# An oscillating memory stage with tokens on partitions: running sums as products, halves of the tokens in turn

## The chip, the cores and the metric

The kernel is one program on one core of a Trainium2 chip. A core has five engines with a queue each: TensorE (PE, matrix products into PSUM), VectorE (DVE), ScalarE (ACT, activation functions), GpSimd (POOL), and SyncE (SP), which issues the transfers here. The engines run side by side and wait for each other through semaphores. The metric is the device time of one execution in microseconds (us); less is better.

## What is computed

The network has two layers, each with a cross attention over a context, a token mixer and a mixture of experts. The stage of this change is the token mixer of the first layer, on 8 sequences of 64 tokens with 256 features:

```python
Bm = x @ W_B + b_B
Cm = x @ W_C + b_C
dt = jax.nn.softplus((x @ W_dt1 + b_dt1) @ W_dt2 + b_dt2)
omega = omega_base * dt
phi = jnp.cumsum(omega, axis=1)
content = Bm * x[..., :STATE]
cphi, sphi = (jnp.cos(phi), jnp.sin(phi))
memory_real = jnp.cumsum(content * cphi, axis=1)
memory_imag = jnp.cumsum(content * sphi, axis=1)
retrieved = Cm * (memory_real * cphi + memory_imag * sphi)
y = retrieved @ W_out + b_out + D * x
```

Its input is the layer norm of the residual stream, its result is added to that stream, and the running sums start anew with each sequence.

## The kernel before

The program is a row of stages (`program`): `xattn0`, `memory0`, `ffn0`, `xattn1`, `attn1_ffn1`. Each stage opens a `Block` in which every engine has its own straight list of instructions; between blocks all engines meet at a barrier. The residual stream `core.x` (`resid` in the trace) and its norm stay in SBUF as [128, 4, 256], with 128 tokens on the partitions and four such tiles.

`memory0` works transposed. `Norm` makes `xn`, TensorE transposes it into `xnT`, and all products give features on partitions and the 512 tokens along the free side, two chunks `c` of 128 features. So every tile of the chain (`z`, `ez`, `poly`, `phi`, `cs`, `sn`, `ci`, `cr`, `mi`, `mr`) is 128 x 1024, and biases are one number per partition. The running sums over tokens are VectorE scans (L699, L709, L715), two each, with `carry` as the factor: 1, and 0 where a sequence begins.

The order is written out by hand. TensorE: step products to t1 (L734), to z (L747), B and C (L741), then, once the cosine's square is there, 24 filler products of the identity (`core.warm`, L100), which compute nothing that is used, and the output product (L757). VectorE: bias onto z, content, then the softplus. That is max(z, 0) + log1p(exp(-|z|)), and the logarithm is a polynomial of e = exp(-|z|) in factors (e + s)^2 + o, five of them (`log1p_factors`). ScalarE makes Abs, Exp and the five squares with a ring of three buffers; VectorE multiplies them up (L688 to L694). Then come omega, the scan to phi, the reduction of phi to (-pi, pi) in six operations (L701 to L705), the products and scans of both parts, and the retrieved value `mr`, which the output product reads as its stationary operand. GpSimd makes `base`, that is D times the norm, plus the output bias, plus the residual. SyncE issues twelve transfers. A product of f32 operands shows in the trace as two records, a transpose as one.

## Time and profile before

| What | us |
|---|---|
| Median of 3 runs | 1106.91 (1106.3 to 1108.91) |
| The profiled execution | 1106.76 |
| Its span, first to last instruction | 1105.1 |
| TensorE busy, whole span | 1005.0 |
| VectorE busy, whole span | 571.0 |
| ScalarE busy, whole span | 498.9 |
| Touched stage, first DMA issue to the end of the last addition | 202.25 to 259.54 |

The span is what the instructions take; the rest of an execution's time lies around it. Busy time says how much an engine did, not whether anybody waited for it. TensorE's busy share is high over the whole span, but not in this stage, so it is the stage's own timeline that has to be read. TensorE's clock has two levels, 1.2 and 2.4 GHz; the views give it as a share of the higher one, 0.50 or 1.00, or between where a stretch holds both.

### The profile page before, as it was taken

How to read it: one execution, taken by the hardware profiler on the slowest of the kernel's cores; microseconds unless marked ns; L12 is line 12 of the kernel's file. 1: busy time of each engine (PE TensorE's matmuls, PEld its weight loads, DVE VectorE, ACT ScalarE, POOL GpSimd, SP SyncE). 2: the span in 40 equal slices, each digit the busy share in tenths (PEclk: the TensorE clock that was granted, in tenths of full speed). 3: DMA queues.
4: the chain of work that ended last, by engine and by line, in shares of the span. 5: the costliest groups of instructions: out<-in, count | busy, mean ns of one | idle time of the engine just before them, and what ended most of it. 6: DMA issues, size and time to landing. Idle time of an engine off the chain costs nothing. (4 is left out here: it accounts for less than half of the span.)

```text
span 1105.1 us, 21134 instructions
## 1 busy us (share of the span) xinstructions
PE 1005.0 (91%) x8866; PEld 858.5 (78%) x8866; DVE 571.0 (52%) x811; ACT 498.9 (45%) x744; POOL 179.2 (16%) x164
## 2 busy tenths in 40 slices
PE   8899999727789999899999999999999998959998
PEld 6788888425469985588989898989898865559997
DVE  4577776495734345665545555454646412572211
ACT  5677776322346645535444444444544313213322
POOL 2000000203414423103030312111111004110000
PEclk9999999868779999999999999999999999879999
DMA  5111200102013204111111102020300005903610
GB/s 168 32 62 46 63 24 3 44 0 62 1 55 90 94 28 153 39 39 39 39 41 36 60 16 76 0 76 2 126 24 1 1 1 162 377 11 115 230 39 20
DMA packets 49396, 68.82 MB, mean 62 GB/s; under 512 B 5792, under 2 KB 40816, under 8 KB 49328
## 3 DMA queue, kind: packets, MB, share of 16 engines
q1 hardware_dynamic: 49328, 67.83, 18.7%
q8 instruction: 53, 0.87, 0.3%
q14 instruction: 15, 0.12, 0.0%
HBM read 67.29 MB, written 0.52 MB: 61 GB/s over the span
## 5 line engine op out<-in xcount | busy, mean ns | idle before, releaser
L1380 ACT ACTIVATE e_pr<-ps,e_negmax 128x1024 f32<-128x1024 f32 x64 | 71.4, 1115 | 171.0 <-DVE e_negmax L1385 164.8
L181 PE MATMUL ps<-f_pT_hi,f_cN_hi 128*128 128x256 f32 x512 | 146.1, 285 | 2.4 <-DVE f_pT_lo L1626 2.4
L181 PE MATMUL ps<-f_pT_hi,f_cN_lo 128*128 128x256 f32 x512 | 145.5, 284 | 0.0
L181 PE MATMUL ps<-f_pT_lo,f_cN_hi 128*128 128x256 f32 x512 | 145.4, 284 | 0.0
L1626 DVE TENSOR_TENSOR f_pT_lo<-ps,f_pT_hi 128x1024 fp32r<-128x1024 f32 x64 | 78.2, 1222 | 78.0 <-ACT f_pT_hi L1581 78.0
L181 PE MATMUL ps<-e_cT_hi,e_qb_hi 128*128 128x512 f32 x256 | 105.5, 412 | 0.0
L404 DVE SCALAR_TENSOR_TENSOR a_u<-ps,a_floor,a_cap 128x1024 f32<-128x1024 f32 x64 | 79.2, 1279 | 45.9 <-PE ps L485 45.9
L181 PEld LDWEIGHTS ps<-f_pT_hi,f_cN_hi 128*128 128x128 f32 x512 | 98.5, 192 | 4.6 <-DVE f_pT_lo L1626 2.6
L181 PE MATMUL ps<-e_cT_hi,e_qb_lo 128*128 128x512 f32 x256 | 100.6, 393 | 0.0
L181 PE MATMUL ps<-e_cT_lo,e_qb_hi 128*128 128x512 f32 x256 | 99.9, 390 | 0.0
L181 PEld LDWEIGHTS ps<-f_pT_lo,f_cN_hi 128*128 128x128 f32 x512 | 98.6, 193 | 1.5
L181 PEld LDWEIGHTS ps<-f_pT_hi,f_cN_lo 128*128 128x128 f32 x512 | 98.6, 193 | 0.0
L1385 DVE TENSOR_REDUCE e_negmax<-ps 128x1 f32<-128x1024 f32 x64 | 78.1, 1220 | 30.9 <-PE ps L181 30.2
L336 ACT ACTIVATE a_pr<-a_u,a_nb 128x1024 f32<-128x1024 f32 x64 | 73.8, 1154 | 44.4 <-DVE a_u L404 43.3
L1581 ACT CAST f_pT_hi<-ps 128x1024 fp32r<-128x1024 f32 x64 | 64.8, 1013 | 53.5 <-PE ps L1654 53.5
L1654 PE MATMUL ps<-ident,e_pr 128*128 128x128 f32 x512 | 66.5, 273 | 13.5 <-DVE f_pT_lo L1626 12.3
L100 PE MATMUL ps<-ident 128*128 128x128 f32 x240 | 40.9, 349 | 35.7 <-ACT b_cs L667 19.7
L1375 POOL TENSOR_TENSOR e_cT_lo<-e_rawT,e_cT_hi 128x512 fp32r<-128x512 f32 x32 | 40.4, 1295 | 193.6 <-ACT e_cT_hi L1563 193.6
L1654 PEld LDWEIGHTS ps<-ident,e_pr 128*128 128x128 f32 x512 | 57.0, 140 | 18.5 <-issue 18.3
L100 PEld LDWEIGHTS ps<-ident 128*128 128x128 f32 x240 | 39.4, 261 | 38.7 <-ACT b_cs L667 20.6
L1549 POOL TENSOR_TENSOR f_cN_lo<-e_raw,f_cN_hi 128x512 fp32r<-128x512 f32 x32 | 43.7, 1398 | 138.5 <-ACT f_cN_hi L1570 138.5
L181 PEld LDWEIGHTS ps<-e_cT_hi,e_qb_lo 128*128 128x128 f32 x256 | 48.0, 188 | 11.1
(360 smaller groups left out, 2137.1 us busy)
## 6 DMA issues: line engine op xcount, KB each, us to landing
k_w<-in_L_ffn_W SPq DMA_DIRECT2D x22, 1024.0 KB, 10.1
a_ctxT<-in_ctxT SPq DMA_DIRECT2D x16, 512.0 KB, 3.7
d_w<-in_L_ffn_w SPq DMA_DIRECT2D x32, 256.0 KB, 2.7
e_rawT<-in_ctxT SPq DMA_DIRECT2D x8, 1024.0 KB, 5.0
e_raw<-in_ctx SPq DMA_DIRECT2D x8, 1024.0 KB, 5.6
e_wq<-in_L_xattn_w_q SPq DMA_DIRECT2D x1, 1024.0 KB, 6.2
e_wk<-in_L_xattn_w_k SPq DMA_DIRECT2D x1, 1024.0 KB, 8.7
g_wv<-in_L_xattn_w_v SPq DMA_DIRECT2D x1, 1024.0 KB, 7.8
```

Source lines behind the costliest of these rows:

```text
L100: self.nc.tensor.matmul(self.bank(bank)[:, 0:P], self.ident[:], self.ident[:], start=True, stop=True)
L181: last = nc.tensor.matmul(out, a[i], b[j], start=start and n == 0, stop=stop and n == 2, skip_group_check=skip)
L336: A.activation(pr[:, n % NP, :], u[:, n % NU, :], ACT.Square, bias=nb[:], scale=HD ** -0.5).then_inc(p_ready, 1)
L404: V.scalar_tensor_tensor(u[:, n % NU, :].rearrange("p (r w) -> p r w", r=RT), core.psum[:, 0:2048].rearrange("p (r w) -> p r w", r=RT)[:, ...
L1375: nc.gpsimd.tensor_tensor(cT[1][:, c, cols], rawT[:, c, cols], cT[0][:, c, cols].bitcast(F32), ALU.subtract).then_inc(t_lo, 1)
L1380: nc.scalar.activation(pr[:, p % NPR, :], core.ps[p % 2][:], ACT.Exp, bias=negmax[:, p:p + 1], accum_out=total[:, p:p + 1]).then_inc(exp_r ...
L1385: nc.vector.tensor_reduce(negmax[:, p:p + 1], core.ps[p % 2][:], AX, ALU.max, negate=True).then_inc(max_ready, 1)
L1549: nc.gpsimd.tensor_tensor(cN[1][:, ks, :], raw[:, ks, :], cN[0][:, ks, :].bitcast(F32), ALU.subtract).then_inc(n_lo, 1)
L1581: nc.scalar.copy(pT[0][:, g, :, P * (p % 2):P * (p % 2) + P], core.ps[2][:].rearrange("p (k n) -> p k n", n=P)).then_inc(pT_hi, 1)
L1626: nc.vector.tensor_tensor(pT[1][:, g, :, cols], core.ps[2][:].rearrange("p (k n) -> p k n", n=P), pT[0][:, g, :, cols].bitcast(F32), ALU.s ...
L1654: last = nc.tensor.transpose(core.ps[2][:, k * P:(k + 1) * P], pr[:, p % NPR, k * P:(k + 1) * P], core.ident[:])
```

## The change

The stage is written with tokens on partitions. The chain's tiles are now [128, 4, 256], and each step is done for two halves `h` of two tiles, that is 512 columns.

- The product to z takes t1 as its stationary operand. The bias is a 65th row of `wdt2`, and t1 gets a 65th row of ones. The biases of B, C and the output are products of a single row of ones with a row of biases repeated for two tiles (`bias`); they open the PSUM sums into which the projections add.
- The three running sums are products with `tri`, a triangle of ones for each of the two sequences in a tile (`running`). Scans and `carry` are gone. Results stay in PSUM and VectorE reads them there.
- Softplus: the leading coefficient goes into `gain`, which ScalarE applies inside the square. VectorE's first step multiplies by e, so the separate ones for offset and lead are gone; max(z, 0) is an operation of its own (`relu`). All squares have buffers.
- Omega and D are rows broadcast over the partitions. The last step of the cosine, 1 - 2s^2, is on ScalarE. A dummy Exp of one column stands ahead of t1 on ScalarE's queue.
- `mr` has tokens on partitions and must be transposed for the output product: four transposes and a ScalarE copy per half.
- TensorE's fillers are 3 ahead of z and 30 behind the phase sums, ahead of the sums of the sine part, not 24 behind the cosine.
- GpSimd does two wide operations for `base`, not three, and makes `tri`. SyncE again issues twelve transfers: step weights, bias rows, D and omega, then wB, wC and wout, each with a semaphore of its own.

Lines with a minus are left out of the diff, since the function of before stands above.

```diff
+        tri, ones, one, dummy = sb("tri", [P, P]), sb("ones", [1, P]), sb("one", [P, 1]), sb("dummy", [P, 1])
+        t1 = sb("t1", [RANK + 1, NT])
...
+        gain = lead ** (1 / (2 * len(factors)))
...
+        wide = lambda name: sb(name, [P, TT, D])
+        relu, ez, poly = wide("relu"), wide("ez"), wide("poly")
+        square = [wide(f"square{i}") for i in range(len(factors))]
...
+        part = lambda v, h: v[:, 2 * h:2 * h + 2, :]
+        sums = lambda i, h: core.bank(i + h).rearrange("p (j d) -> p j d", d=D)
...
+            sp.dma_start(wdt2[0:RANK, :], a["L0_attn_W_dt2"]).then_inc(dt_in, 16)
+            sp.dma_start(wdt2[RANK:RANK + 1, :], a["L0_attn_b_dt2"].partition_broadcast(1)).then_inc(dt_in, 16)
             sp.dma_start(bdt1[:], a["L0_attn_b_dt1"]).then_inc(dt_in, 16)
...
+            for i, src in enumerate(("B", "C", "out")):
+                sp.dma_start(rows[:, i, :], a["L0_attn_b_" + src].partition_broadcast(1)).then_inc(rows_in, 16)
+            for dst, src in ((skip, "D"), (omega, "omega_base")):
+                sp.dma_start(dst[:], a["L0_attn_" + src].partition_broadcast(P)).then_inc(e_in, 16)
+            for w, src, done in ((wB, "B", b_in), (wC, "C", c_in), (wout, "out", o_in)):
+                sp.dma_start(w[:], a["L0_attn_W_" + src].rearrange("(c p) o -> p c o", p=P)).then_inc(done, 16)
...
+            step(g.memset(tri[:], 1.0))
+            step(g.affine_select(out=tri[:], in_=tri[:], compare_op=ALU.is_ge, fill=0.0, base=0,
+                                 pattern=[[1, P]], channel_multiplier=-1))
+            g.memset(tri[0:T, T:P], 0.0).then_inc(rows_ready, 1)
...
+            pool.wait_ge(e_in, 32)
+            step(g.tensor_tensor(base[:], xn[:], bc(skip[:], 1, TT), ALU.mult))
+            g.tensor_tensor(base[:], base[:], x[:], ALU.add).then_inc(base_ready, 1)
...
+            A.activation(dummy[:], core.ident[:, 0:1], ACT.Exp)
+            act.wait_ge(dt_in, 64)
             act.wait_ge(t1_psum, 1)
...
+            A.activation(t1[0:RANK, :], core.bank(2)[0:RANK, :], ACT.Identity, bias=bdt1[:]).then_inc(t1_ready, 1)
+            act.wait_ge(const, len(factors) + 1)
+            for h in range(HALVES):
+                act.wait_ge(z_psum, h + 1)
+                A.activation(part(ez, h), sums(0, h), ACT.Abs).then_inc(ez_abs, 1)
+            for h in range(HALVES):
+                act.wait_ge(ez_abs, h + 1)
+                A.activation(part(ez, h), part(ez, h), ACT.Exp, scale=-1.0).then_inc(ez_ready, 1)
+                act.wait_ge(ez_ready, h + 1)
+                for i in range(len(factors)):
+                    A.activation(part(square[i], h), part(ez, h), ACT.Square, bias=shift[:, i:i + 1],
+                                 scale=gain).then_inc(square_ready, 1)
+            for h in range(HALVES):
+                act.wait_ge(r_ready, h + 1)
+                A.activation(part(sn, h), part(phi, h), ACT.Sin).then_inc(sn_ready, 1)
+                A.activation(part(half, h), part(phi, h), ACT.Sin, scale=0.5).then_inc(half_ready, 1)
+                act.wait_ge(half_ready, h + 1)
+                A.activation(part(half, h), part(half, h), ACT.Square).then_inc(half_squared, 1)
+                act.wait_ge(half_squared, h + 1)
+                A.activation(part(cs, h), part(half, h), ACT.Identity, bias=one[:], scale=-2.0).then_inc(cs_ready, 1)
+            for h in range(HALVES):
+                act.wait_ge(retT_psum, h + 1)
+                A.copy(retT[:, :, 2 * P * h:2 * P * h + 2 * P],
+                       core.bank(h).rearrange("p (c n) -> p c n", c=DC)).then_inc(retT_ready, 1)
...
+            def softplus(h):
+                for i, (_, offset) in enumerate(factors):
+                    dve.wait_ge(square_ready, N * h + i + 1)
+                    step(V.scalar_tensor_tensor(part(poly, h), part(square[i], h), offset * gain * gain,
+                                                part(ez if i == 0 else poly, h), ALU.add, ALU.mult))
+                step(V.tensor_tensor(part(poly, h), part(poly, h), part(relu, h), ALU.add))
+                V.tensor_tensor(part(poly, h), part(poly, h), bc(omega[:], 1, 2), ALU.mult).then_inc(w_ready, 1)
+            def reduce(h):
+                dve.wait_ge(phi_psum, h + 1)
+                step(V.tensor_scalar(part(turns, h), sums(2, h), 1.0 / TWO_PI, MAGIC, ALU.mult, ALU.add))
+                step(V.tensor_scalar(part(turns, h), part(turns, h), MAGIC, None, ALU.subtract))
+                for i, size in enumerate((PI_A, PI_B, PI_C)):
+                    step(V.scalar_tensor_tensor(part(phi, h), part(turns, h), -size,
+                                                sums(2, h) if i == 0 else part(phi, h), ALU.mult, ALU.add))
+                V.tensor_scalar(part(phi, h), part(phi, h), 3.1415925, -3.1415925, ALU.min, ALU.max
+                                ).then_inc(r_ready, 1)
+            def imaginary(h):
+                dve.wait_ge(sn_ready, h + 1)
+                V.tensor_tensor(part(ci, h), part(content, h), part(sn, h), ALU.mult).then_inc(ci_ready, 1)
+            def real(h):
+                dve.wait_ge(cs_ready, h + 1)
+                V.tensor_tensor(part(cr, h), part(content, h), part(cs, h), ALU.mult).then_inc(cr_ready, 1)
+            def sine_part(h):
+                dve.wait_ge(mi_psum, h + 1)
+                step(V.tensor_tensor(part(mi, h), sums(4, h), part(sn, h), ALU.mult), False)
+            def retrieve(h):
+                dve.wait_ge(mr_psum, h + 1)
+                step(V.tensor_tensor(part(mr, h), sums(0, h), part(cs, h), ALU.mult))
+                step(V.tensor_tensor(part(mr, h), part(mr, h), part(mi, h), ALU.add))
+                dve.wait_ge(c_psum, h + 1)
+                V.tensor_tensor(part(mr, h), sums(6, h), part(mr, h), ALU.mult).then_inc(ret_ready, 1)
             norm.vector(dve, step)
...
+            dve.wait_ge(e_in, 32)
+            for h in range(HALVES):
+                dve.wait_ge(ez_abs, h + 1)
+                step(V.tensor_scalar(part(relu, h), sums(0, h), 0.0, None, ALU.max), False)
+            softplus(0)
+            softplus(1)
+            for h in range(HALVES):
+                dve.wait_ge(b_psum, h + 1)
+                step(V.tensor_tensor(part(content, h), sums(4, h), part(xn, h), ALU.mult), h == 1)
+            reduce(0)
+            reduce(1)
+            imaginary(0)
+            real(0)
+            imaginary(1)
+            sine_part(0)
+            real(1)
+            retrieve(0)
+            sine_part(1)
+            retrieve(1)
             dve.wait_ge(base_ready, 1)
...
+            def tile(i, j):
+                return core.bank(i + j // 2)[:, D * (j % 2):D * (j % 2) + D]
+            def bias(bank, i):
+                t.matmul(core.bank(bank), ones[:], bc(rows[:, i, :], 1, 2), start=True,
+                         stop=False, skip_group_check=True)
+            def project(first, lhsT, w, j):
+                for c in range(DC):
+                    last = t.matmul(tile(first, j), lhsT[:, c, j * P:(j + 1) * P], w[:, c, :], start=False,
+                                    stop=c == DC - 1, skip_group_check=True)
+                return last
+            def running(first, v, h):
+                for j in (2 * h, 2 * h + 1):
+                    last = t.matmul(tile(first, j), tri[:], v[:, j, :], start=True, stop=True)
+                return last
             norm.tensor(pe)
...
+            pe.wait_ge(dt_in, 64)
             for c in range(DC):
...
+                last = t.matmul(core.bank(2)[0:RANK, :], wdt1[:, c, :], xnT[:, c, :], start=c == 0, stop=c == DC - 1)
             last.then_inc(t1_psum, 1)
...
+            pe.wait_ge(rows_ready, 3)
+            core.warm(7, 3)
+            pe.wait_ge(t1_ready, 1)
+            for j in range(TT):
+                last = t.matmul(tile(0, j), t1[:, j * P:(j + 1) * P], wdt2[:], start=True, stop=True)
+                if j % 2:
+                    last.then_inc(z_psum, 1)
+            pe.wait_ge(rows_in, 48)
+            for h in range(HALVES):
+                bias(4 + h, 0)
+                bias(6 + h, 1)
+            pe.wait_ge(b_in, 16)
+            for j in range(TT):
+                last = project(4, xnT, wB, j)
+                if j % 2:
+                    last.then_inc(b_psum, 1)
+            pe.wait_ge(c_in, 16)
+            for j in range(TT):
+                last = project(6, xnT, wC, j)
+                if j % 2:
+                    last.then_inc(c_psum, 1)
+            for h in range(HALVES):
+                pe.wait_ge(w_ready, h + 1)
+                running(2, poly, h).then_inc(phi_psum, 1)
+            core.warm(0, 30)
+            for h in range(HALVES):
+                pe.wait_ge(ci_ready, h + 1)
+                running(4, ci, h).then_inc(mi_psum, 1)
+                pe.wait_ge(cr_ready, h + 1)
+                running(0, cr, h).then_inc(mr_psum, 1)
+            for h in range(HALVES):
+                bias(2 + h, 2)
+            pe.wait_ge(o_in, 16)
+            def transposes(h):
+                pe.wait_ge(ret_ready, h + 1)
                 for c in range(DC):
...
+                    for j in range(2):
+                        last = t.transpose(core.bank(h)[:, P * (2 * c + j):P * (2 * c + j) + P],
+                                           mr[:, 2 * h + j, c * P:(c + 1) * P], core.ident[:])
+                last.then_inc(retT_psum, 1)
+            def output(h):
+                pe.wait_ge(retT_ready, h + 1)
+                for j in (2 * h, 2 * h + 1):
+                    last = project(2, retT, wout, j)
+                last.then_inc(y_psum, 1)
+            for h in range(HALVES):
+                transposes(h)
+                output(h)
```

On TensorE, from the t1 product on, the order before was this (`b_wdt` is W_dt1 or W_dt2, `ident` with no second name a filler):

```order
L734 MATMUL ps<-xnT,b_wdt 64x512
L747 MATMUL ps<-b_t,b_wdt 128x512 [waits b_t1_ready]
L747 MATMUL ps<-b_t,b_wdt 128x512
L741 MATMUL ps<-xnT,b_wB 128x512 [waits b_w_in]
L741 MATMUL ps<-xnT,b_wB 128x512 x3
L741 MATMUL ps<-xnT,b_wC 128x512 x4
L100 MATMUL ps<-ident 128x128 [waits b_half_squared]
L100 MATMUL ps<-ident 128x128 x23
L757 MATMUL ps<-b_wout,b_mr 128x256 [waits b_ret_ready]
L757 MATMUL ps<-b_wout,b_mr 128x256 x7
```

In the changed kernel the piece from B's products to the first output product is this:

```order
L772 MATMUL ps<-b_wB,xnT 128x256 [waits b_b_in]
L772 MATMUL ps<-b_wB,xnT 128x256 x7
L772 MATMUL ps<-b_wC,xnT 128x256 [waits b_c_in]
L772 MATMUL ps<-b_wC,xnT 128x256 x7
L778 MATMUL ps<-b_poly,b_tri 128x256 [waits b_w_ready]
L778 MATMUL ps<-b_poly,b_tri 128x256
L778 MATMUL ps<-b_poly,b_tri 128x256 [waits b_w_ready]
L778 MATMUL ps<-b_poly,b_tri 128x256
L100 MATMUL ps<-ident 128x128 x30
L778 MATMUL ps<-b_ci,b_tri 128x256 [waits b_ci_ready]
L778 MATMUL ps<-b_ci,b_tri 128x256
L778 MATMUL ps<-b_cr,b_tri 128x256 [waits b_cr_ready]
```

Running sums stand between C and the output, and the fillers stand behind the phase sums with no wait of their own, in front of the first sum of `ci`.

On VectorE, from the sine part to the end of the stage, the order before was this:

```order
L707 TENSOR_TENSOR b_ci<-b_content,b_sn 128x1024 [waits b_sn_ready]
L709 SCALAR_TENSOR_TENSOR b_mi<-b_carry,b_ci 128x512 [waits b_dve_step] x2
L712 TENSOR_SCALAR b_cs<-b_cs 128x1024 [waits b_half_squared,b_dve_step]
L713 TENSOR_TENSOR b_cr<-b_content,b_cs 128x1024 [waits b_dve_step]
L715 SCALAR_TENSOR_TENSOR b_mr<-b_carry,b_cr 128x512 [waits b_dve_step] x2
L716 TENSOR_TENSOR b_mi<-b_mi,b_sn 128x1024 [waits b_dve_step]
L717 TENSOR_TENSOR b_mr<-b_mr,b_cs 128x1024 [waits b_dve_step]
L718 TENSOR_TENSOR b_mr<-b_mr,b_mi 128x1024 [waits b_dve_step]
L721 SCALAR_TENSOR_TENSOR b_mr<-ps,b_bC,b_mr 128x512 [waits b_c_psum,b_dve_step]
```

In the changed kernel it is this, twelve operations in all:

```order
L717 TENSOR_TENSOR b_ci<-b_content,b_sn 128x512 [waits b_sn_ready]
L721 TENSOR_TENSOR b_cr<-b_content,b_cs 128x512 [waits b_cs_ready]
L717 TENSOR_TENSOR b_ci<-b_content,b_sn 128x512 [waits b_sn_ready]
L725 TENSOR_TENSOR b_mi<-ps,b_sn 128x512 [waits b_mi_psum]
L721 TENSOR_TENSOR b_cr<-b_content,b_cs 128x512 [waits b_cs_ready]
L729 TENSOR_TENSOR b_mr<-ps,b_cs 128x512 [waits b_mr_psum]
L730 TENSOR_TENSOR b_mr<-b_mr,b_mi 128x512 [waits b_dve_step]
L732 TENSOR_TENSOR b_mr<-ps,b_mr 128x512 [waits b_c_psum,b_dve_step]
```

The six scans of 512 columns are gone from VectorE, the halves interleave, and four of these operations now wait for a sum from TensorE.

## Rows read from the trace of the kernel before

**Rows 1.** Timeline, 207 to 220: start, length, engine, line, operation [idle before].

```profile
207.28 1.04 PE L171 MATMUL ps<-ident,xn 128*128 128x128 f32 x8
...
208.36 0.58 ACT L163 COPY xnT<-ps 128x512 f32<-128x512 f32 x1 [3.80 <-PE ps L171]
208.36 0.69 DVE L148 COPY xnT<-ps 128x512 f32<-128x512 f32 x1 [1.58 <-PE ps L171]
...
211.13 0.68 ACT L651 ACTIVATE b_t<-ps,b_bdt 64x512 f32<-64x512 f32 x1 [2.19 <-PE ps L734]
...
211.87 1.98 PE L747 MATMUL ps<-b_t,b_wdt 64*128 64x512 f32 x4 [0.83 <-ACT b_t L651]
...
213.10 1.54 DVE L677 TENSOR_SCALAR b_z<-ps,b_bdt 128x512 f32<-128x512 f32 x2 [4.05 <-PE ps L747]
...
214.67 1.06 ACT L653 ACTIVATE b_ez<-b_z 128x1024 f32<-128x1024 f32 x1 [2.85 <-DVE b_z L677]
...
215.74 1.28 ACT L655 ACT_TABLE_LOAD   x1
...
217.04 1.06 ACT L655 ACTIVATE b_ez<-b_ez 128x1024 f32<-128x1024 f32 x1
217.31 3.60 PE L741 MATMUL ps<-xnT,b_wC 128*128 128x512 f32 x8
...
218.13 5.31 ACT L661 ACTIVATE b_square<-b_ez,b_shift 128x1024 f32<-128x1024 f32 x5
...
219.41 0.69 DVE L688 TENSOR_SCALAR b_poly<-b_square 128x1024 f32<-128x1024 f32 x1 [1.06 <-ACT b_square L661]
```

**Rows 2.** Timeline of VectorE, 220 to 252.

```profile
220.43 5.00 DVE L690 SCALAR_TENSOR_TENSOR b_poly<-b_square,b_poly 128x1024 f32<-128x1024 f32 x4 [0.32 <-ACT b_square L661]
...
228.51 1.23 DVE L699 TENSOR_TENSOR_SCAN b_phi<-b_carry,b_z 128x512 f32<-128x512 f32 x1
229.77 0.48 DVE L698 TENSOR_SCALAR b_z<-b_z,b_omega 128x512 f32<-128x512 f32 x1
...
250.66 1.41 DVE L721 SCALAR_TENSOR_TENSOR b_mr<-ps,b_bC,b_mr 128x512 f32<-128x512 f32 x2
```

**Rows 3.** Timeline, the engines that wait and the stage's end, 237 to 259.

```profile
237.51 1.06 ACT L664 ACTIVATE b_sn<-b_phi 128x1024 f32<-128x1024 f32 x1 [12.77 <-DVE b_phi L705]
...
240.65 7.46 PE L100 MATMUL ps<-ident 128*128 128x128 f32 x48 [19.74 <-ACT b_cs L667]
...
252.12 6.69 PE L757 MATMUL ps<-b_wout,b_mr 128*128 128x256 f32 x16 [4.01 <-DVE b_mr L721]
256.01 0.69 DVE L726 TENSOR_TENSOR resid<-b_base,ps 128x512 f32<-128x512 f32 x1 [3.94 <-PE ps L757]
258.85 0.69 DVE L726 TENSOR_TENSOR resid<-b_base,ps 128x512 f32<-128x512 f32 x1 [2.15 <-PE ps L757]
```

**Rows 4.** Timeline of TensorE in other stages: work that follows a pause.

```profile
10.06 0.47 PE L181 MATMUL ps<-a_ctx_hi,a_wkv_hi 128*128 128x512 f32 x1 [1.84 <-DVE a_ctx_lo L387]
...
198.77 2.48 PE L520 MATMUL ps<-a_wo,a_oT 128*128 128x256 f32 x8 [2.76 <-DVE a_oT L414]
...
882.53 0.39 PE L181 MATMUL ps<-f_pT_hi,f_cN_hi 128*128 128x256 f32 x1 [2.36 <-DVE f_pT_lo L1626]
...
966.30 1.99 PE L1932 MATMUL ps<-h_wo,h_prod 128*128 128x256 f32 x8 [0.23 <-POOL h_prod L1827]
```

**Rows 5.** Windows: stretch, length, busy time (records) per engine, PEclk, DMA share, GB/s.

```profile
11.00:13.00 2.00, 2.00 (x10) 1.58 (x10) 0.78 (x6) 1.26 (x2) 0.00 (x0) 1.00 0.97 209
...
201.00:202.00 1.00, 0.25 (x1) 0.00 (x0) 0.69 (x1) 0.00 (x0) 0.00 (x0) 0.50 0.00 0
...
252.00:253.00 1.00, 0.88 (x2) 0.79 (x3) 0.07 (x1) 0.00 (x0) 0.00 (x0) 0.50 0.00 0
...
883.00:884.00 1.00, 1.00 (x7) 1.00 (x7) 0.00 (x0) 0.00 (x0) 0.00 (x0) 0.50 0.00 0
...
966.30:968.30 2.00, 1.99 (x8) 1.44 (x8) 1.72 (x2) 0.00 (x0) 0.16 (x1) 1.00 0.77 246
```

More of the change, by code:

```diff
@@ L597, in memory0 @@
+        rows = sb("rows", [1, 3, D])
+        omega, skip = sb("omega", [P, D]), sb("skip", [P, D])
+        tri, ones, one, dummy = sb("tri", [P, P]), sb("ones", [1, P]), sb("one", [P, 1]), sb("dummy", [P, 1])
+        t1 = sb("t1", [RANK + 1, NT])
         lead, factors = log1p_factors()
+        gain = lead ** (1 / (2 * len(factors)))
         shift = sb("shift", [P, len(factors)])
[L599 to L601 removed]
+        wide = lambda name: sb(name, [P, TT, D])
@@ L658, in _ @@
-            for i in range(len(factors)):
-                if i >= NSQ:
-                    act.wait_ge(square_used, i - NSQ + 1)
-                nc.scalar.activation(flat(square[i % NSQ]), flat(ez), ACT.Square,
-                                     bias=shift[:, i:i + 1]).then_inc(square_ready, 1)
-            act.wait_ge(r_ready, 1)
-            nc.scalar.activation(flat(sn), flat(phi), ACT.Sin).then_inc(sn_ready, 1)
-            nc.scalar.activation(flat(half), flat(phi), ACT.Sin, scale=0.5).then_inc(half_ready, 1)
@@ L767 @@
+            for h in range(HALVES):
+                transposes(h)
+                output(h)
 class Gate:
```

152 lines of the change are left out of this document (30 added, 122 removed).

## Prediction

> **What bounds the kernel now.** I read four views. First, time and spans: the profiled execution took 1106.76 us, 1105.1 of it span, and the median of the runs is 1106.91, so a sum made against the profile is carried to the median by adding 0.15. Second, the timeline of the stage that the diff touches, which runs from about 202 to 259.54 us. It has a block of its own, with a barrier at either end, so what it saves comes off the span one for one, unless the stages behind it change. Its front [rows 1] is a relay, one engine at work and the others waiting: TensorE's step products begin at 211.87, VectorE adds the bias from 213.10, ScalarE takes Abs from 214.67, loads a table (1.28), takes Exp from 217.04, and the squares start at 218.13. The polynomial can only start at 219.41. From there to 252.07 (250.66 and 1.41 long) VectorE is the bound [rows 2]: 32.66 us, nearly gapless; ScalarE waits 12.77 us for it [rows 3]. Then comes a tail [rows 3]: TensorE gets `mr` only now, finds its clock at the lower level (0.50, that is 1.2 GHz [rows 5]), and needs until 258.85 to release the last addition, which ends at 259.54. Third, the granted clock by stretches [rows 5], since most of what is added is TensorE work. Fourth, how TensorE's clock stood after its earlier pauses [rows 4, 5]. No engine waits for a DMA on this path: each release in these rows is by an engine.
>
> **Durations I use.** A VectorE operation of 1024 f32 columns takes 1.23 us, and so does a scan of only 512 columns [rows 2]; one of 512 columns that isn't a scan takes 0.69, also with a PSUM operand, as in L726 and the copy in L148 [rows 3, 1]. Between dependent ones lie 0.03 (229.74 to 229.77 [rows 2]). So half a tile costs 0.72. A one-input operation in SBUF takes 0.69 for 1024 columns (L688) and 0.48 for 512 with an operand per partition (L698); without that operand I take half the streaming, 0.43, so 0.46 with the gap [rows 1, 2]. ScalarE: 1.06 for 1024 columns and 0.58 for a copy of 512, so Abs or Exp of a half is about 0.63 and a square with its shift operand 0.71 (between 0.58 and the five squares' 5.31 in all) [rows 1]. TensorE at the full clock: four products of 512 columns in 3.60, so 0.86 each and 0.43 for 256 columns; four of 256 columns, start to last result, 1.99 with the clock at 1.00 [rows 1, 4, 5]; eight transposes 1.04, 0.27 alone, so four in 0.66 [rows 1]. A hop between engines is 0.04.
>
> **Part 1, the front.** Removed from the relay are VectorE's bias addition (the bias is a 65th row of the product), the table load (the dummy Exp asks for it early) and half of Abs, Exp and the square, since the first half of the tokens goes ahead. The first half is again 512 columns of product, so Abs starts at 213.10, where VectorE's read did; Abs 0.63, then the second half's Abs (its product is 0.86 later, 213.95 to 214.58), Exp to 215.24, first square to 215.98, polynomial from 216.01. That is 3.40 us earlier than 219.41. What hides the rest: three filler products and GpSimd's constants lie under the wait for t1. The dummy's load starts when ScalarE's copy is done, 208.94, and with 1.28 and some 0.2 for the activation it is over at 210.4, before t1's product is read at 211.13.
> The Trainium skill, "ScalarE: Activation LUTs", section "What ACT_TABLE_LOAD costs", speaks against this edit: it puts a switch at about 2.66 us, a drain included. Here the load in L655 lies between Abs, which ended at 215.73, and Exp at 217.04, so 1.31 in all [rows 1], and the trace does not agree for such a case. By the page the dummy would end at 211.8 and t1 would be 0.7 later.
>
> **Part 2, VectorE's chain.** The offset, lead and bias operations go into other ones, the six scans go to TensorE, the cosine's last step to ScalarE, all else in halves. Counted from the changed order, in slots of 0.72 and 0.46: softplus 2 x 7 x 0.72 = 10.08; content 2 x 0.72 = 1.44; range reduction 2 x (4 x 0.72 + 2 x 0.46) = 7.60; then twelve products and additions, 8.64. Together 27.76, from 216.01 to 243.77. Before it was 32.66, so 4.90 saved. For that nobody may keep VectorE waiting. The ScalarE squares come every 0.62, faster than 0.72. TensorE runs z, four single-row bias products, B and C back to back, 0.86 x (2 + 4 + 4 + 4) = 12.0, to 223.9, then the phase sum of half 0, result at about 225.1; VectorE asks for it at 227.53 (216.01 + 10.08 + 1.44): slack 2.4. Half 1's weights are ready at 226.1, its sum at 227.3, asked for at 231.3. After the reduction ends at 235.13, the sine of half 0 is long there (since 231.3 plus four ScalarE steps of about 0.65), so ci and cr follow at once; ci's running sum, 235.9 + 1.2, is asked for at 237.3; cr's, 1.1 after VectorE's cr, likewise in time. The cosine of half 1 is ready at about 237.7, asked for at 238.0. All slacks are small but positive with TensorE at its full clock.
>
> **Part 3, the tail.** `mr` of half 0 is ready at 235.13 + 8 x 0.72 = 240.89. TensorE though has the last cr (ready 238.73, so 239.63) and then two bias products of 0.86 in its queue: free at 241.35, so this costs 0.4. Transposes to 242.01, ScalarE's copy to 242.63, output of half 0 read at 244.7. TensorE turns to half 1 at 244.39: transposes to 245.05, copy to 245.67, output 1.99 to 247.70, addition to 248.43. Before, the tail from 252.07 to 259.54 was 7.47; now, from 243.77, it is 4.66: 2.81 saved, though 8 transposes and 2 copies are new, because half 0 is under half 1's VectorE work and the clock is taken to be high.
>
> **Part 4, the clock.** The thirty fillers start behind the last phase sum at about 227.1 and have 128 columns each, a quarter of 0.86, so 30 x 0.22 = 6.6 and a little more (the 24 of before took 7.46 over both levels [rows 3]), to about 233.9. ci is ready at 235.9: a pause of about 2.1. Rows bound what that does: after a pause of 1.84 the clock stayed at 1.00; after one of 2.76 it was 0.50 some two us on, and after one of 2.36 likewise [rows 4, 5]. I am between. If it falls, the sums and the biases run part of their 5.2 us at half speed, and I put the cost at up to 1.7, all of it on the tail, where TensorE is late already. I take half, 0.85, since it will fall in some executions.
>
> **Sum.** 3.40 + 4.90 + 2.81 = 11.11, less 0.85, is 10.26: 1106.76 - 10.26 = 1096.5 profiled, 1096.7 as the median. The stage behind starts 10 us earlier with the same work and, as before, a high clock.
>
> **Unknown costs, both ends.** No row shows a product with one or 65 rows on the contraction side, or one whose moving operand repeats a row: between 0 and twice the 0.86 of rows 1. The first four are covered by the 2.4 slack, so at twice they cost 3.4 - 2.4 = 1.0; the last two 1.7. I take 0.86, as a product's time in all rows goes by columns. VectorE reading PSUM together with an SBUF tensor: 0.69 in L726, 0.75 where a pointer is added (1.41 for two in L721, overlapping [rows 2]): 0 to 0.06 on some 14 operations, so up to 0.8; I take 0.
>
> **Rivals.**
> A, TensorE becomes the bound (the other side). It decides if the clock is at 1.2 GHz from the step products on. Then z, biases, B and C take 24 us, to 236; the sums 3.4, thirty fillers 12.9 in front of ci, to 252.3; eight sums and two biases 10.3, to 262.6; and a tail of some 11.7 (two transposes and copies of 1.8, output 3.9 as in 252.12 to 256.01 [rows 3], 3.4 more, the addition): 274.3, which is 14.8 late: 1121.7. With the clock falling only at the fillers it is about 1109.9. Against it: the step products and C of before ran at the full rate [rows 1], with pauses around them like those of now. For it: the fillers stand in a queue ahead of needed work. 2 in 100.
> B, single-row products are dear: 1.0 + 1.7 on top, 1099.4. 7 in 100.
> C, the early table load reaches t1: by rows, its end at 210.4 plus a stall of as much again as the load gives 211.7, so t1 is 0.6 late and all with it: 1097.3. The page of the Trainium skill named in part 1 speaks for it. 7 in 100.
> D, the savings are there but the next stage gives some back: its clock moves between levels too, and the runs of before lie 2.6 us apart (1106.3 to 1108.91). The time would be 1098 to 1100. 12 in 100.
> E, the change doesn't do what it says and ScalarE has to reload tables between Sin and Square or Identity, twice per half, 4 x 1.28 in part hidden: 1099 to 1102. Before, Square followed Exp without a load [rows 1], and the changed order shows one load only, ahead of the first Sin. 2 in 100.
>
> **How the numbers follow.** My forecast, with the clock falling or not (1095.8 to 1097.6), has 70 in 100. To hold 8 in 10 I take in B, C and most of D: 1094.3 to 1100.0; the lower end leaves 1.5 for hops that overlap better than I charge. What a measurement can tell is about 0.3%, 3.3 us: faster means under 1103.6, which only A does not reach and an unlucky D or E nearly misses: faster 0.95, same 0.03, slower 0.02.
>
> **What would show it.** Right: the first polynomial operation near 216.0; no table load between Abs and Exp; `b_turns` at 227.5 with no wait; VectorE without idle time over 0.3 from 216 to 243.8; the last addition ending at 248.4 to 250.2, followed by the same norm. Wrong: a VectorE wait on TensorE at a running sum (TensorE or its clock is the bound), single-row products over 0.9 each, t1 after 211.2, or stages behind this one that grow by more than 1 us.

## The result, and the profile after the change

The changed kernel took 1101.8 us (median of 1099.39 to 1103.26), the kernel before 1106.65 (1104.47 to 1109.89): a ratio of 0.995, 95% interval 0.9928 to 0.9972, or 4.85 us less. The interval leaves out 1, so the kernel is faster, but its time is above the range that I gave (1094.3 to 1100.0). Two later comparisons of the same two kernels, below, gave ratios of 0.9909 and 0.9931, and 1099.06 and 1099.88 us for the changed one: just inside the range. The profiled execution of the changed kernel took 1100.49 us, 1098.8 of it span: 6.3 less span than before.

The timeline of the stage, all engines, in the changed kernel; columns as in [rows 1]. These lines answer to [rows 1 to 3].

```profile
207.87 1.04 PE L171 MATMUL ps<-ident,xn 128*128 128x128 f32 x8
...
209.55 1.28 ACT L663 ACT_TABLE_LOAD   x1
...
209.69 1.93 PE L784 MATMUL ps<-xnT,b_wdt 128*64 128x512 f32 x4 [0.78 <-DVE xnT L148]
...
210.84 0.20 ACT L663 ACTIVATE b_dummy<-ident 128x1 f32<-128x1 f32 x1
...
211.72 0.68 ACT L666 ACTIVATE b_t<-ps,b_bdt 64x512 f32<-64x512 f32 x1 [0.67 <-PE ps L784]
...
212.45 1.99 PE L790 MATMUL ps<-b_wdt,b_t 65*128 65x256 f32 x8
...
214.37 4.43 PE L767 MATMUL ps<-b_rows,b_ones 1*128 1x512 f32 x8
214.38 1.43 DVE L738 TENSOR_SCALAR b_relu<-ps 128x512 f32<-128x512 f32 x2 [4.74 <-ACT b_ez L670]
...
216.38 0.69 DVE L700 SCALAR_TENSOR_TENSOR b_poly<-b_square,b_ez 128x512 f32<-128x512 f32 x1 [0.58 <-ACT b_square L676]
...
218.73 6.32 PE L772 MATMUL ps<-b_wB,xnT 128*128 128x256 f32 x16
...
224.89 3.62 PE L772 MATMUL ps<-b_wC,xnT 128*128 128x256 f32 x16
...
226.31 1.28 DVE L743 TENSOR_TENSOR b_content<-ps,xn 128x512 f32<-128x512 f32 x2
...
228.35 1.89 PE L778 MATMUL ps<-b_poly,b_tri 128*128 128x256 f32 x8
229.48 0.69 DVE L707 TENSOR_SCALAR b_turns<-ps 128x512 f32<-128x512 f32 x1 [1.89 <-PE ps L778]
...
230.07 6.86 PE L100 MATMUL ps<-ident 128*128 128x128 f32 x60
...
237.62 1.13 PE L778 MATMUL ps<-b_ci,b_tri 128*128 128x256 f32 x4 [0.69 <-DVE b_ci L717]
...
241.41 1.98 PE L767 MATMUL ps<-b_rows,b_ones 1*128 1x512 f32 x4
...
244.30 0.69 DVE L732 TENSOR_TENSOR b_mr<-ps,b_mr 128x512 f32<-128x512 f32 x1
...
244.65 3.59 PE L772 MATMUL ps<-b_wout,b_retT 128*128 128x256 f32 x8 [0.68 <-ACT b_retT L688]
...
249.35 1.99 PE L772 MATMUL ps<-b_wout,b_retT 128*128 128x256 f32 x8 [0.67 <-ACT b_retT L688]
251.39 0.69 DVE L757 TENSOR_TENSOR resid<-b_base,ps 128x512 f32<-128x512 f32 x1 [2.35 <-PE ps L772]
...
252.39 2.92 PE L100 MATMUL ps<-ident 128*128 128x128 f32 x24 [1.04 <-PEq L586]
```

Read it downwards. The front is shorter, as meant: no load stands between Abs and Exp, and from the start of the step products (212.45) to the first polynomial operation (216.38) it is 3.93, before it was 7.54 [rows 1]. Then something that [rows 2] don't have: VectorE waits 1.89 for TensorE at `b_turns`. TensorE was late because the 16 products of B took 6.32 where the 16 equal ones of C, right behind them, took 3.62. In the tail the same work comes twice: the output's first half took 3.59, its second 1.99. The granted clock (the third column from the right) says why:

```profile
213.00:216.00 3.00, 3.00 (x11) 1.79 (x10) 1.38 (x2) 2.08 (x4) 2.92 (x2) 1.00 0.05 14
216.00:218.00 2.00, 2.00 (x5) 0.56 (x3) 1.55 (x3) 2.00 (x4) 0.50 (x1) 0.80 0.00 0
218.00:224.00 6.00, 6.00 (x13) 4.21 (x13) 5.76 (x9) 5.78 (x9) 0.00 (x0) 0.50 0.00 0
224.00:226.00 2.00, 2.00 (x11) 1.75 (x10) 1.90 (x4) 0.00 (x0) 0.00 (x0) 0.99 0.00 0
...
241.00:244.00 3.00, 2.98 (x11) 1.16 (x9) 2.93 (x5) 0.00 (x0) 0.00 (x0) 1.00 0.00 0
...
245.00:247.00 2.00, 2.00 (x6) 1.54 (x6) 0.00 (x0) 0.00 (x0) 0.00 (x0) 0.50 0.00 0
...
248.00:252.00 4.00, 2.67 (x14) 1.80 (x12) 1.30 (x2) 0.58 (x1) 0.00 (x0) 1.00 0.00 0
```

The clock fell from 2.4 to 1.2 GHz between 216 and 218, while TensorE was busy the whole length of each window and had been since 209.69. What it had been doing since 214.37 is the four single-row bias products. It fell again between 244 and 245, after the output's two single-row products (241.41); there four transposes and a pause of 0.68 lie between.

**The stage.** I measure it from the first filler of its normalization to the first filler of the next: 57.56 us before (202.30 to 259.86), 48.96 now (203.43 to 252.39), so 8.60 less. The code ahead of the stage, the same in both kernels, took 1.13 more in this execution, the code behind it 1.17 more. What is left is the 6.3 of the span.

### The profile page after: what moved, and what is told of

It reads as the page before. It is cut to its first block and busy times, and to the rows that moved or that the text cites. A ratio compares the mean times of both kernels' runs of the same rounds, so it can differ in the third digit from the quotient of the medians.

```text
span 1098.8 us, 21327 instructions
## 1 busy us (share of the span) xinstructions
PE 1022.7 (93%) x8948; PEld 873.8 (80%) x8948; DVE 564.7 (51%) x820; ACT 503.5 (46%) x759; POOL 177.5 (16%) x167
## 5 line engine op out<-in xcount | busy, mean ns | idle before, releaser
L404 DVE SCALAR_TENSOR_TENSOR a_u<-ps,a_floor,a_cap 128x1024 f32<-128x1024 f32 x64 | 79.2, 1279 | 45.8 <-PE ps L485 45.8
L181 PEld LDWEIGHTS ps<-e_cT_lo,e_qb_hi 128*128 128x128 f32 x256 | 48.4, 189 | 8.5
L181 PEld LDWEIGHTS ps<-e_cT_hi,e_qb_hi 128*128 128x128 f32 x256 | 48.2, 188 | 8.7 <-issue 0.7
```

What stands on the lines that cost most here:

```text
L181: last = nc.tensor.matmul(out, a[i], b[j], start=start and n == 0, stop=stop and n == 2, skip_group_check=skip)
L404: V.scalar_tensor_tensor(u[:, n % NU, :].rearrange("p (r w) -> p r w", r=RT), core.psum[:, 0:2048].rearrange("p (r w) -> p r w", r=RT)[:, ...
```

## The experiments

My theory after the result: a product with one row on the contraction side keeps TensorE busy but doesn't keep its clock, and this, not the columns it streams, is what it costs. The rivals: the fall is a draw that comes or not (the clock moved in before's stages too); something else in the new order (the fillers, the pause ahead of ci) does it; the loss is behind the stage. "The stage" below is measured as above. Its opening stretch, from the first filler to the step products, took 9.02 to 9.62 us from trace to trace, with the old code as with the new; where 0.6 us matter, I count from the step products on.

**e1_rows128: the bias products over 128 rows, the bias in each.**

```diff
-        rows = sb("rows", [1, 3, D])
+        rows = sb("rows", [P, 3, D])
...
-        tri, ones, one, dummy = sb("tri", [P, P]), sb("ones", [1, P]), sb("one", [P, 1]), sb("dummy", [P, 1])
+        tri, ones, one, dummy = sb("tri", [P, P]), sb("ones", [P, P]), sb("one", [P, 1]), sb("dummy", [P, 1])
...
-                sp.dma_start(rows[:, i, :], a["L0_attn_b_" + src].partition_broadcast(1)).then_inc(rows_in, 16)
+                sp.dma_start(rows[:, i, :], a["L0_attn_b_" + src].partition_broadcast(P)).then_inc(rows_in, 16)
...
-            g.memset(ones[:], 1.0).then_inc(rows_ready, 1)
+            g.memset(ones[:], 1.0 / P).then_inc(rows_ready, 1)
```

> The changed kernel, but each bias product has all 128 rows: the bias is in every partition and the stationary operand is 1/128. Same columns, same records, same sum. Theory A (TensorE's single-row products, though it is busy, let its clock fall): no stretch at 0.50 between 212 and 230, B's 16 records take about 3.5 us and not 6.32, VectorE waits under 0.3 at b_turns and not 1.89, the first output half takes about 2.0 and not 3.59, and the stage (first filler of its norm to the first of the next) takes about 45.5 us and not 48.96. Theory B (the clock falls for the pauses and the kind of work around, not for the rows): B again about 6.3, the stage about 49.

Measured: 1099.33 us (before 1107.44), ratio 0.992 (0.9908 to 0.9933); stage 49.06. The clock did what the theory says: bias products 3.60, B 3.62. The time didn't, for another reason. The three broadcasts of 128 partitions stand ahead of `b_omega` in the queue, so GpSimd's base operations began late and ran beside the polynomial:

```profile
216.42 2.37 POOL L656 TENSOR_TENSOR b_base<-xn,b_skip 128x1024 f32<-128x1024 f32 x1 [10.03 <-DMA b_omega<-in_L_attn_omega_base]
```

```profile
217.99 1.35 DVE L700 SCALAR_TENSOR_TENSOR b_poly<-b_square,b_ez 128x512 f32<-128x512 f32 x1 [0.43 <-ACT b_square L676]
219.37 4.92 DVE L700 SCALAR_TENSOR_TENSOR b_poly<-b_square,b_poly 128x512 f32<-128x512 f32 x4
```

VectorE needed 1.35 and 4.92 for what took 0.69 and 2.87 (timeline of this run, GpSimd and VectorE). TensorE then paused 3.51 ahead of the second phase sum, its clock fell there, and the fillers took 8.63.

**e2_rowszero and e11_rowszero_again: 128 rows, 127 of them zeros.** `rows` and `ones` have 128 partitions as in e1, but the DMA is one row again, so the base operations begin early.

```diff
+            sp.wait_ge(zeroed, 1)
...
-                sp.dma_start(rows[:, i, :], a["L0_attn_b_" + src].partition_broadcast(1)).then_inc(rows_in, 16)
+                sp.dma_start(rows[0:1, i, :], a["L0_attn_b_" + src].partition_broadcast(1)).then_inc(rows_in, 16)
...
+            g.memset(rows[:], 0.0).then_inc(zeroed, 1)
```

> The changed kernel, but each bias product has 128 rows of which 127 hold zeros in the moving operand. Theory A in the form that the rows taking part count: as with all rows filled, B about 3.5 us, the stage about 45.5. In the form that what is multiplied counts: as in the changed kernel, B about 6.3, stage about 49. Theory B: about 49 as well.

> The changed kernel with the bias products over 128 rows (127 of them zeros), as e2_rowszero, a second time and beside the changed kernel on the same chip. If the fall of the clock hangs on the single-row products: the four front bias products 3.6 us, the products of B behind them 3.6 us, no wait at b_turns, the output's halves 1.99 us each, the stage (first filler of the normalization to first filler of the next) 45.8 us within 0.5, 3 us shorter than the changed kernel's, the whole time near 1095. If e2_rowszero was a lucky draw of the clock: the stage lies at 48 to 49.5 us and the products of B at 6.3 to 6.8 in this run too.

**e8_after_again and e12_after_beside: the changed kernel itself again,** e12 on the chip of e11.

> The changed kernel again, for a second trace of it and a time beside the others. If the single-row products act each time: a stretch at 0.50 between 214 and 226 with B over 5 us, stage 48 to 50 us, ratio to before about 0.995. If the first trace was chance: B 3.6 and the stage under 47. What lies behind the stage differs between traces by the clock alone: 844 to 847.5 us from the next stage's first filler to the end.

> The changed kernel as it is, on the same chip as e11_rowszero_again. If the fall of the clock hangs on the single-row products: B's products 6.3 to 6.8 us, the wait at b_turns 1.9, the stage 48.9 to 49.5 us, the whole time 1098 to 1102. If it is a draw: B's products at 3.6 us and a stage near 46 in one of its traces.

Measured: 1094.93 us, 0.9884 (0.987 to 0.9899), and 1095.29, 0.9895 (0.9871 to 0.9918), with 128 rows; the changed kernel 1099.06, 0.9909 (0.988 to 0.9937), and 1099.88, 0.9931 (0.9908 to 0.9953). Stages: 45.77 and 45.73 against 49.40 and 48.85. The timeline of TensorE, with one line of VectorE, in e11_rowszero_again, then in e12_after_beside:

```profile
214.11 3.60 PE L770 MATMUL ps<-b_rows,b_ones 128*128 128x512 f32 x8
...
216.22 1.21 DVE L703 SCALAR_TENSOR_TENSOR b_poly<-b_square,b_ez 128x512 f32<-128x512 f32 x1 [0.58 <-ACT b_square L679]
...
217.55 3.62 PE L775 MATMUL ps<-b_wB,xnT 128*128 128x256 f32 x16
...
236.12 1.13 PE L781 MATMUL ps<-b_ci,b_tri 128*128 128x256 f32 x4 [1.50 <-DVE b_ci L720]
...
239.82 1.88 PE L770 MATMUL ps<-b_rows,b_ones 128*128 128x512 f32 x4
...
242.81 1.99 PE L775 MATMUL ps<-b_wout,b_retT 128*128 128x256 f32 x8 [0.68 <-ACT b_retT L691]
```

```profile
214.00 3.82 PE L767 MATMUL ps<-b_rows,b_ones 1*128 1x512 f32 x8
217.75 5.24 PE L772 MATMUL ps<-b_wB,xnT 128*128 128x256 f32 x16
...
227.42 0.69 DVE L707 TENSOR_SCALAR b_turns<-ps 128x512 f32<-128x512 f32 x1 [0.20 <-PE ps L778]
...
239.34 1.98 PE L767 MATMUL ps<-b_rows,b_ones 1*128 1x512 f32 x4
...
243.00 3.78 PE L772 MATMUL ps<-b_wout,b_retT 128*128 128x256 f32 x8 [0.68 <-ACT b_retT L688]
```

The columns, the repeated moving operand and the order are the same; only the rows of the two operands differ, and 127 of zeros in the moving one are enough. Which of the operands counts is not separated, since both got their 128 rows together. From the step products to the last addition of e11 the clock did not leave 2.4 GHz, and VectorE has no wait at `b_turns`:

```profile
212.30:248.60 36.30, 31.45 (x161) 24.82 (x160) 28.95 (x44) 16.05 (x25) 4.50 (x2) 1.00 0.01 4
```

That window is of e11_rowszero_again, the columns as above. The single-row products cost the stage 3.1 to 3.6 us; counted from the step products on, it is 39.27 to 40.03 in the changed kernel's three traces against 36.15 and 36.67, so 2.6 to 3.9. Where they cost it varies: in e12 the clock was back during B (5.24), the wait at `b_turns` was 0.20 and not the 1.89 that I expected, and nearly all of the loss was in the tail, 8.11 from the last `mr` to the last addition against 5.14 in e11. And e11 was not free of trouble: GpSimd's second base operation reached to 216.87, and the first polynomial operation took 1.21 and not 0.69. A draw as the cause of the fall in the front is ruled out as far as these traces go: in the four with single-row products in the front (the changed kernel three times, e4 below) B took 5.24 to 6.78; in the six with 128 rows there (e1, e2, e5, e6, e7, e11) and in e3 without them it took 3.62. The Trainium skill, "TensorE: Matmul & The Clock Gate", section "Part 1: The HAM clock gate", has the clock follow how busy TensorE has been. The trace does not agree for products of one row, since TensorE was busy without a pause from 209.69 on and the clock still fell between 216 and 218.

**e3_nobias: the bias products left out.** The biases of B, of C and of the output are missing from what this kernel computes.

```diff
-                    last = t.matmul(tile(first, j), lhsT[:, c, j * P:(j + 1) * P], w[:, c, :], start=False,
+                    last = t.matmul(tile(first, j), lhsT[:, c, j * P:(j + 1) * P], w[:, c, :], start=c == 0,
...
-            for h in range(HALVES):
-                bias(4 + h, 0)
-                bias(6 + h, 1)
...
-            for h in range(HALVES):
-                bias(2 + h, 2)
```

> The changed kernel without the six bias products; the biases of B, C and the output are left out of the result, and the projections open their sums. Theory A: B about 3.5 us at the full clock, TensorE 3.4 + 1.7 us less to do, the stage about 45 us; little below the variant with 128 rows, since the first four are then covered. Theory B: the clock falls as before, B about 6.3 but 3.4 earlier, VectorE's wait at b_turns gone, the first output half still 3.6, stage about 46.5.

Measured: 1095.63 us, 0.9895 (0.9881 to 0.991); stage 45.35. Leaving the products out gains no more than 0.4 over giving them 128 rows: at the full clock they are as good as free here. TensorE paused 3.83 ahead of the second phase sum, lost its clock (fillers 8.26), and had it back before ci.

**e5_first_four: 128 rows in the front only,** one row for the output's two.

```diff
-                t.matmul(core.bank(bank), ones[:], bc(rows[:, i, :], 1, 2), start=True,
+                k = 1 if i == 2 else P
+                t.matmul(core.bank(bank), ones[0:k, :], bc(rows[0:k, i, :], 1, 2), start=True,
```

> Only the four bias products ahead of B and C have 128 rows (127 of zeros); the two ahead of the output stay single-row. If each group of single-row products costs by letting the clock fall: no 0.50 and B at 3.62 us in front, VectorE's wait at b_turns (1.89) gone; the output's first half at 3.59 or 1.99 us according to whether the clock falls behind 1.7 us of single-row products and the pause for ScalarE's copy. Stage 45.8 to 47.4 us against 48.96 with all single-row and 45.77 with none, so the front group carries at least half of the 3.2. Rival: the groups only matter together, stage about 49.

Measured: 1096.95 us, 0.9896 (0.9862 to 0.9931); stage 50.33. The front is clean, the tail is not (TensorE's timeline):

```profile
239.55 1.98 PE L771 MATMUL ps<-b_rows,b_ones 1*128 1x512 f32 x4
241.46 0.89 PE L828 MATMUL ps<-ident,b_mr 128*128 128x128 f32 x4
243.03 3.78 PE L776 MATMUL ps<-b_wout,b_retT 128*128 128x256 f32 x8 [0.68 <-ACT b_retT L691]
...
248.34 3.78 PE L776 MATMUL ps<-b_wout,b_retT 128*128 128x256 f32 x8 [0.67 <-ACT b_retT L691]
```

So two products of 0.9 us each can be enough, and here both halves of the output ran at 1.2 GHz: 4.6 more than e2. My expectation of 45.8 to 47.4 for this stage was wrong: the front's repair alone gave nothing in this trace. Stage and whole time disagree in this run: the median is better than the changed kernel's, the profiled stage worse. How long the low clock lasts differs between executions, and one trace shows one of them.

**e4_nofill and e6_zero_nofill: without the thirty fillers,** once with single-row products, once with 128 rows.

```diff
-            core.warm(0, 30)
```

> The changed kernel without the thirty fillers behind the phase sums. If the fillers hold the clock as intended: the clock is 0.50 from the sine sums on, sums and output products at half speed, the stage 3 to 5 us longer than 48.96. If the clock is anyway lost to the single-row output biases: under 2 us longer.

> All bias products with 128 rows and the thirty fillers taken out. If the fillers are what holds the clock to the sine sums: the sums start at 0.50, 2.08 and 1.91 us in place of 1.13 and 1.03, VectorE waits some 1.4 us for them, the stage is 46.8 to 48.5 us against 45.77. Rival: with full rows ahead the clock outlasts the pause of about 8 us: stage 45.8.

Measured: e4 1102.89 us, 0.9949 (0.9929 to 0.9969), stage 49.59, B 6.78 and the wait at `b_turns` 1.89 as with fillers; e6 1099.12, 0.992 (0.9894 to 0.9945), stage 47.86. The fillers don't cause the fall. The two runs differ by 1.7 us of stage (1.4 from the step products on), near the 1.89 that VectorE waits at `b_turns` in e4; the output ran at the full clock in both, so this is about the price of the front alone. The fillers are worth 2.1 us of the stage once the rows are mended (47.86 against 45.77; 2.6 from the step products on), since without them TensorE pauses until ci and its sums start low:

```profile
235.25 2.07 PE L781 MATMUL ps<-b_ci,b_tri 128*128 128x256 f32 x4 [8.19 <-DVE b_ci L720]
237.11 1.91 PE L781 MATMUL ps<-b_cr,b_tri 128*128 128x256 f32 x4
```

In e4 the clock had only just risen when the output's single-row products came, and both halves of the output took 1.99: one case of five in which such products did not bring it down before the stage was over. Why it held is not shown.

**e7_best: the output's bias added by GpSimd** in `base`, a third wide operation there; 128 rows for the rest.

```diff
-            for h in range(HALVES):
-                bias(2 + h, 2)
...
+            pool.wait_ge(bout_in, 16)
+            g.tensor_tensor(base[:], base[:], bc(bout[:], 1, TT), ALU.add).then_inc(base_ready, 1)
```

> Bias products of B and C with 128 rows; the output bias is added by GpSimd in base, as before the change, so TensorE has no bias products ahead of the transposes. They started at 240.74 right behind TensorE's queue in the variant with 128 rows; VectorE's first retrieved half is ready some 0.7 earlier. Stage about 45.1 us against 45.77, time 1094 to 1095. Rival: without these 1.9 us of TensorE work the clock falls in the tail and the stage is 46 to 48.

Measured: 1098.55 us, 0.9907 (0.9872 to 0.9942); stage 48.31, where I had expected 45.1: worse than e2. The rival that I had named, a fall of the clock in the tail without this TensorE work, came. Timelines of VectorE and of GpSimd:

```profile
217.41 2.67 DVE L706 SCALAR_TENSOR_TENSOR b_poly<-b_square,b_ez 128x512 f32<-128x512 f32 x1 [0.58 <-ACT b_square L682]
```

```profile
217.18 2.36 POOL L663 TENSOR_TENSOR b_base<-b_base,b_bout 128x1024 f32<-128x1024 f32 x1
```

VectorE's 0.69 us operation took 2.67, on the critical path: it ended at 220.08, 0.54 after GpSimd's, which had begun 0.23 ahead of it. The Trainium skill, "SBUF — State Buffer", section "SBUF: two separate sides", says that a VectorE operation with two SBUF inputs and a GpSimd operation that reads SBUF exclude each other, the later one waiting for the whole of the earlier; the trace agrees. TensorE's timeline, and the granted clock over three stretches (columns as above):

```profile
229.46 1.13 PE L784 MATMUL ps<-b_poly,b_tri 128*128 128x256 f32 x4 [2.79 <-DVE b_poly L709]
...
244.95 3.17 PE L778 MATMUL ps<-b_wout,b_retT 128*128 128x256 f32 x8 [0.68 <-ACT b_retT L694]
```

```profile
230.00:237.00 7.00, 7.00 (x62) 6.95 (x61) 6.66 (x13) 2.47 (x4) 0.00 (x0) 1.00 0.00 0
...
245.00:246.00 1.00, 1.00 (x4) 0.86 (x5) 0.97 (x2) 0.00 (x0) 0.00 (x0) 0.81 0.00 0
246.00:247.00 1.00, 1.00 (x3) 0.79 (x3) 0.15 (x1) 0.00 (x0) 0.00 (x0) 0.50 0.00 0
```

Two things follow. A pause of 2.79 ahead of the second phase sum did not lower the clock. And in the tail, behind pauses of 1.49, 1.01 and 0.68, it fell with no single-row product there at all. So single-row products are not the only way to lose it in the tail: with them it fell in four traces of five, without them in one of six (in e7, not in e1, e2, e3, e6 and e11). In the front, the count is four of four against none of seven.

**e9_before_warm42 and e10_before_dummy: the kernel before with one part each,** 42 fillers instead of 24 ahead of its output, or the early dummy Exp alone.

```diff
-            core.warm(2, 24)
+            core.warm(2, 42)
```

```diff
+            nc.scalar.activation(dummy[:], core.ident[:, 0:1], ACT.Exp)
```

> The kernel of before with 42 fillers in place of 24 behind the cosine, so that they end at about 252 and not 248.1, nothing else. If the low clock of the output is worth what the tail's rows say: its 16 records take 3.5 us and not 6.69, the last addition is 3 us earlier, stage 54.4 us against 57.56, time 3 us less. Rival: fillers reach past the retrieved value's arrival and give part back, 1 to 2 us less.

> The kernel of before with only the dummy Exp ahead of t1, so the table is loaded early. The load of 1.28 us between Abs and Exp goes and t1 starts no later: stage 56.3 us against 57.56, time 1.3 us less. Rival C of the prediction (the load reaches t1): 0.6 or more given back, stage 56.9 or longer.

Measured: e9 1106.7 us, 0.9975 (0.9961 to 0.999), stage 54.04, the 16 products of the output 3.72 instead of 6.69 [rows 3]. So 3.0 us of the old stage (6.69 less 3.72) were its clock in the tail, and fillers alone could have had them; the other 0.5 of the 3.5 is the opening stretch. The median shows 1.85 less than before beside it. e10 1107.79, 0.9996 (0.9976 to 1.0015), stage 55.03, with no load between Abs and Exp. The polynomial began 1.02 earlier behind the step products (6.52 against 7.54), and 1.5 of the stage's 2.5 less is not the dummy's but the output's, 5.19 and not 6.69, at a clock that was back sooner. Behind the stage that trace took 850.5 against 845.2 before, so the stage's gain doesn't show in the whole.

**Behind the stage.** The code there is the same in all kernels, yet its length is not: 843.0 to 850.5. One place tells most of it, the gate's product at the start of the mixture (TensorE's timeline of the changed kernel, then of the same kernel as e8_after_again):

```profile
305.72 3.56 PE L913 MATMUL ps<-d_gate_w,c_mlaT 128*128 128x8 f32 x16 [1.03 <-PEq L1204]
```

```profile
308.38 1.92 PE L913 MATMUL ps<-d_gate_w,c_mlaT 128*128 128x8 f32 x16 [1.03 <-PEq L1204]
```

Where it took 3.56 (the changed kernel, e5, e10, e12) the mixture was 103.6 to 104.6 long, elsewhere 101.7 to 102.2. It happens with and without the change, and in one kernel both ways, so I put it down to where the clock stands at that moment; what decides that stays open. It came in three of the five traces with single-row products in the tail, in none of the six changed ones without them, and in one of the three of the old kernel: a link with this stage is neither shown nor ruled out by so few. The last part behaves likewise: from the fillers of the last stage to the end it is 125.8 to 125.9 us where these fillers took 5.46 (before, e9, e10 and e12) and 123.5 to 124.1 where they took 4.3 to 4.7 (the rest). So some 5 us of the whole time are drawn behind this stage, and a single trace of two kernels can't be subtracted without looking at these places first.

## Why the prediction was right and wrong

| | predicted | changed kernel | the same, e12 | e11, 128 rows |
|---|---|---|---|---|
| stage start to step products | 0 | -0.55 | +0.01 | -0.51 |
| step products to first polynomial operation | -3.40 | -3.61 | -3.61 | -3.60 |
| VectorE's chain to the last `mr` | -4.90 | -4.05 | -5.75 | -5.39 |
| tail, with part 4's 0.85 | -1.96 | -0.38 | +0.64 | -2.33 |
| stage | -10.26 | -8.60 | -8.71 | -11.83 |

Each entry is a length less that of before: 7.54 for the second line, 32.66 and 7.47 for the third and fourth [rows 1 to 3]. The changed kernel's chain runs from 216.38 to 244.99 and its tail to 252.08. The first line isn't the change's: in e12 that stretch was 9.58, in the first trace of the same kernel 9.02, before 9.57. So 0.55 of the -8.60 is luck.

**Part 1 was right**, to 0.2. Its rule of hops and half-size durations held. **Rival C did not come**: the dummy was over at 211.04 and t1 began at 211.72, 0.67 after its product, as in every such hop. The load took 1.28, so the 2.66 of the Trainium skill's page named in part 1 was not seen.

**Part 2 was right in its slots and wrong in its slack.** Without the wait the chain is 26.72, predicted 27.76. The slack of 2.4 ahead of `b_turns` rested on twelve full-clock products, 12.0 us from the step products to the end of C. They took 16.06 (212.45 to 228.51): the four bias products 0.8 more than 3.60, B 2.7 more.

**Part 3 was right with the clock up**: e11's tail is 5.14, predicted 4.66, the changed kernel's 7.09. The output's first half alone ran 1.6 long, and its retT copy, transposes and addition came after it in line.

**Part 4 looked at the wrong cause.** The pause ahead of ci was 0.69, since the late phase sums pushed the fillers back, and the clock stayed. With 128 rows the pause is 1.49 to 1.50, shorter than my 2.1, and the clock stayed as well. The bounds of that part don't hold: pauses of 3.51 and 3.83 lost it, but one of 2.79 kept it (e7), longer than the 2.36 and 2.76 that had lost it in the kernel before [rows 4], so the length of one pause doesn't decide it. The fall in the front came with no pause at all.

**The step that failed is "Unknown costs", and with it part 2's slack of 2.4 and part 3's high clock, which leaned on it.** I saw that no row showed a product with one row, and bounded it by its own duration, 0 to twice 0.86. Its own duration was indeed near that (4.43 for four, 1.98 for two). The cost was in the products behind it: B's 16 at half the rate, the output's eight at half the rate. Rival B had the right object and the wrong mechanism: it priced the products' own length at 2.7 us, where that grew by 0.8 and 0.1 (4.43 and 1.98 against 3.60 and 1.88) and the loss behind them made 3.1 to 3.6 of the stage, so that its price is near is luck. Rival A, with TensorE as the bound, came true for 1.89 us at one place. Two of my own signs of being wrong came too: a VectorE wait at a running sum, and single-row products over 0.9 each.

**In the stage, the miss is smaller than this cost.** It is 1.66 (8.60 against 10.26), since the rest came out better than forecast: in e11 by 1.57, from the opening stretch (0.51), a shorter front and chain (0.20 and 0.49) and the tail (0.37, with the 0.85 for the clock, which wasn't needed).

**The rest of the miss is D's.** That is the larger part, some 3.5 of the 5.1 us between 1096.7 and 1101.8: 1.13 ahead of the stage, where D did not look, 1.17 behind it, and 1.3 between this trace and the median. With -8.60 in the stage, my own sum gives 1106.76 - 8.60 + 0.15 = 1098.3. The first comparison gave 1101.8, with the mixture's start at the low clock in its trace; the two later ones 1099.06 and 1099.88. My range allowed for either cause alone, not for both.

**The version to use** is e2_rowszero: 1094.93 and 1095.29 us, 12.5 and 13.3 us less than before beside it, 4.6 less than the changed kernel on the same chip. Of that difference the stage's traces show 3.1; the traces of e11 and e12 also differ by 4.1 us behind the stage, where the code is the same.

## What to carry over

A product that adds a bias from one row is nearly free in columns, but a few in a row can bring TensorE's clock down for what follows; here it paid to give it all 128 rows, with zeros in 127, by one memset off the path. When no row shows a new form of instruction, bound not only its duration but what it does to the work behind it. Before moving work to GpSimd, look for what VectorE does with two SBUF inputs in those microseconds: here a GpSimd operation of 2.36 us cost 1.98 on the path.

## What the runs showed of the hardware

- Single-row products keep TensorE busy and not its clock: 1.00 before them, 0.50 from 218 to 224 with TensorE busy throughout. Zeros in the moving operand don't matter: 127 zero rows keep the clock as well as 128 full ones (B 3.62 in e2 and in e1). The products over 65 rows (212.45) lasted only 1.99 in all and no fall followed them in seven traces; a longer row of them, and numbers of rows between 1 and 65, were not tried.
- After two of them (1.98 us) it fell in four traces of five, not in e4; in e7 it fell in the same place without them.
- TensorE's pauses and its clock: behind single pauses of 1.84 and 2.79 it stayed up, behind 2.36, 2.76, 3.51 and 3.83 it was down.
- VectorE and GpSimd beside each other on SBUF: 0.69 became 2.67, and four operations of 2.87 in all became 4.92.
